# The FFN gate is computed in the preparation, and each super-tile is finished while the next one runs

## The reference

```
    g = _silu(_L0_ffn_ref(xn, L0_ffn_weight, L0_ffn_bias))
    x = x + s * g
```

## Time and profile before

| | |
|---|---|
| median of the runs | 1339.04 us |
| the profiled execution | 1338.07 us |
| its span, first to last instruction | 1336.3 us |
| mean granted TensorE clock | 0.952 |
| VectorE busy | 1224.1 us, 92% of the span |
| TensorE matmuls busy | 1133.7 us, 85% |
| ScalarE busy | 797.7 us, 60% |
| GpSimd busy | 728.3 us, 55% |

### The profile page before, as it was taken

One profiled execution on the slowest core, in us unless ns is written; L12 is line 12 of the kernel. 1 busy time (PEld: TensorE's weight loads), 2 busy tenths in 40 slices (PEclk: granted clock), 3 DMA queues, 4 the chain that ended last, 5 costly groups with the idle time before them and its releaser, 6 DMA issues. The chain is left out here.

```text
span 1336.3 us, 30910 instructions
## 1 busy us (share of the span) xinstructions
PE 1133.7 (85%) x11514; PEld 832.9 (62%) x11514; DVE 1224.1 (92%) x1945; ACT 797.7 (60%) x1226; POOL 728.3 (55%) x562
## 2 busy tenths in 40 slices
PE   4873999989999999999999999899999999999810
PEld 3742666666666666666676666666766666667600
DVE  7774999989998999999998999899989999999688
ACT  5732666656666666666666666666666666666432
POOL 4001566656665566556664666566655665666523
PEclk9865999999999999999999999999999999999955
DMA  7535332343221422342223323342224323222033
GB/s 185 176 98 127 73 73 65 69 93 85 65 65 44 106 66 66 68 112 66 63 63 74 81 66 68 66 113 57 60 51 112 66 65 69 61 57 60 19 100 89
DMA packets 68513, 105.66 MB, mean 79 GB/s; under 512 B 14051, under 2 KB 32716, under 8 KB 68044
## 3 DMA queue, kind: packets, MB, share of 16 engines
q1 hardware_dynamic: 68364, 103.68, 33.2%
HBM read 24.73 MB, written 9.96 MB: 26 GB/s over the span
## 5 line engine op out<-in xcount | busy, mean ns | idle before, releaser
L1189 POOL TENSOR_TENSOR rot<-part 128x512 f32<-128x512 f32 x256 | 382.5, 1494 | 531.9 <-DVE part L1026 480.4
L1026 DVE SCALAR_TENSOR_TENSOR part<-bcs,k_prmT,trig 128x512 f32<-128x512 f32 x512 | 500.5, 1028 | 1.4 <-DMA trig<-tri 1.3
L1138 ACT ACTIVATE E<-d 128x512 f32<-128x512 f32 x256 | 151.7, 592 | 184.1 <-PE d L846 181.5
L864 PE MATMUL s<-rot 64*128 64x128 f32 x2048 | 149.7, 285 | 23.6 <-POOL rot L1189 19.1
L1044 DVE TENSOR_TENSOR M<-s,E 128x512 f32<-128x512 f32 x256 | 163.5, 678 | 2.4 <-PE s L864 1.8
L864 PEld LDWEIGHTS s<-rot 64*128 64x128 f32 x2048 | 126.9, 188 | 62.0 <-issue 54.6
L1198 POOL TENSOR_TENSOR ce<-rot,eb 128x512 f32<-128x512 f32 x128 | 160.1, 1272 | 3.0 <-ACT eb L1160 3.0
L1220 POOL TENSOR_TENSOR sqa<-sqa,sq 128x512 f32<-128x512 f32 x112 | 142.5, 1272 | 14.2 <-ACT sq L1143 6.2
L956 PE MATMUL y<-M,xk 128*64 128x128 f32 x2048 | 140.1, 279 | 0.0
L878 PEld LDWEIGHTS o<-k_w_o,yT 128*128 128x128 f32 x1024 | 132.5, 191 | 10.4 <-DVE yT L1103 5.0
L878 PE MATMUL o<-k_w_o,yT 128*128 128x128 f32 x1024 | 134.5, 275 | 2.6 <-DVE yT L1103 2.6
(11 more groups left out here) (234 smaller groups left out, 1792.8 us busy)
## 6 DMA issues: line engine op xcount, KB each, us to landing
trig<-tri SPq DMA_DIRECT2D x512, 128.0 KB, 2.4
bcs<-bc_t SPq DMA_DIRECT2D x16, 256.0 KB, 4.0
bcs<-bc_t SPq DMA_DIRECT2D x32, 128.0 KB, 3.9
a_big<-in_L_attn_u SPq DMA_DIRECT2D x4, 512.0 KB, 6.0
xn_t<-a_xnT SPq DMA_DIRECT2D x1, 2048.0 KB, 16.4
tc_t<-a_tcT SPq DMA_DIRECT2D x1, 2048.0 KB, 15.9
bc_t<-a_tmp SPq DMA_DIRECT2D x1, 2048.0 KB, 7.5
tcs<-tc_t SPq DMA_DIRECT2D x8, 256.0 KB, 3.0
```

Of the source, the lines that this page charges most:

```text
L864: last = nc.tensor.matmul(Sp[j][:, k], rot[rows, q % 2, p, 0, k], rot[rows, q % 2, p, 1, k], start=True, stop=True)
L1026: nc.vector.scalar_tensor_tensor(out=part[:, 2 * p + f, :], in0=bcs[:, (t + q // NQ) % 2, 2 * w + f, :], scalar=col, in1=trig[:, p, 1 - f, ...
L1138: nc.scalar.activation(E[:, h % 2, :], Dp[:], ACT.Exp).then_inc(e_ready, 1)
L1189: nc.gpsimd.tensor_tensor(rot[:, q % 2, p, w, :], part[:, 2 * p, :], part[:, 2 * p + 1, :], ALU.add).then_inc(rot_ready, 1)
```

## The change

Three things change.

1. `prepare` makes the gate. VectorE takes the extremes of `xnT` and of the FFN weight between its other steps; TensorE and VectorE make the scales; the weight is quantised; at the end of the stage the eight super-tiles are scaled (ScalarE), quantised (VectorE), multiplied with the bias added by a matmul (TensorE) and put through Silu (ScalarE), and SyncE stores each gate in a DRAM tensor. The stage ends when the last gate has landed.
2. `units` finishes super-tile `t - 1` in groups 0 and 1 of super-tile `t`. The mean of squares is made and its root taken (VectorE `norm_start`, ScalarE `root`, VectorE `norm_seeded`, GpSimd `norm_refined`), ScalarE scales the projected result out of PSUM (`normalised`) in the place of the two copies, GpSimd multiplies by the gate and adds `u` (`finished`), SyncE stores in group 2 and loads the next gate and the next `u` in group 4. The last super-tile is finished behind the loop, with the last two products on VectorE. The two reductions of `xn` at `q == 2` are gone.
3. `finish` is gone, and with it the tiles `s_acc`, `ssq` and `mags`.

```diff
@@ prepare, sync
+            for t in range(NS):
+                sp.wait_ge(g_done, t + 1)
+                sp.dma_start(gate_d[t], fgate[:, t % 2, :]).then_inc(gate_stored[t % 2], 16)
             sp.wait_ge(masks_stored, 16 * 7)
+            for i in range(2):
+                sp.wait_ge(gate_stored[i], 16 * NS // 2)
@@ prepare, tensor
+            pe.wait_ge(am_done, 2)
+            nc.tensor.transpose(ps_x[1][0:2, 0:P], am[:], ident[:]).then_inc(am_t, 1)
             for g in range(4, 8):
                 linear(g)
+            pe.wait_ge(am2_done, 1)
+            nc.tensor.matmul(ps_x[1][:, 2 * P:2 * P + 2], ones[0:2, 0:P], am2[:, 0:2], start=True, stop=True).then_inc(sc_t, 1)
...
+            pe.wait_ge(left, 2)
+            for t in range(NS):
+                b = ps[2 + t % 2]
+                if t >= 2:
+                    pe.wait_ge(g_done, t - 1)
+                nc.tensor.matmul(b[:], ones[0:1, :], bias4[:], start=True, stop=False, skip_group_check=True)
+                pe.wait_ge(xq_done, t + 2)
+                for c in range(CS):
+                    last = nc.tensor.matmul(b[:, c * P:c * P + P], xq[:, t % 2, c * P:c * P + P], wq[:], start=False,
+                                            stop=c == CS - 1, skip_group_check=True)
+                last.then_inc(g_t, 1)
@@ prepare, vector
+            def extreme(b, op):
+                i = 0 if op == ALU.max else 1
+                link(nc.vector.tensor_reduce(peak[:, i, b:b + 1], xnT[:, b * L:(b + 1) * L], AX.X, op))
             for g in range(0, 8, 2):
                 dve.wait_ge(bc_squared, g + 1)
                 nc.vector.tensor_copy(big[:, 512 * g:512 * g + 512], ps[B_BANK[g]][:]).then_inc(bc_copied_v, 1)
+                extreme(g // 2, ALU.max)
...
+            extreme(0, ALU.min)
+            extreme(1, ALU.min)
             dve.wait_ge(stored[1], 16)
             dve.wait_ge(bc_done, BATCH)
             link(nc.vector.tensor_tensor(pr, big3[:, :, 0:N], big3[:, :, N:2 * N], ALU.mult))
+            dve.sem_inc(pr_done, 1)
+            extreme(2, ALU.min)
+            extreme(3, ALU.min)
...
+            link(nc.vector.tensor_scalar(sc[:, 0:2], ps_x[1][:, 2 * P:2 * P + 2], 1e-12, None, ALU.max))
+            link(nc.vector.reciprocal(sc[:, 0:2], sc[:, 0:2]))
+            link(nc.vector.tensor_scalar(sc[:, 0:2], sc[:, 0:2], FP8_MAX, None, ALU.mult))
...
+            dve.wait_ge(w_scaled, 2)
+            quantise(wq[:], wv[:, 0, :], wv[:, 1, :], P)
...
-            link(nc.vector.tensor_reduce(K["mags"][:, 2 * NS:2 * NS + 1], stage2[:, 10 * P:11 * P], AX.X, ALU.max))
-            link(nc.vector.tensor_reduce(K["mags"][:, 2 * NS + 1:2 * NS + 2], stage2[:, 10 * P:11 * P], AX.X, ALU.min))
+            for t in range(NS):
+                dve.wait_ge(xq_done, t + 1)
+                dve.wait_ge(x_scaled, 2 * t + 2)
+                if t >= 2:
+                    dve.wait_ge(g_t, t - 1)
+                quantise(xq[:, t % 2, :], fv[:, t % 2, :], fmag[:, t % 2, :], ST)
@@ prepare, scalar
+            def gate_input(t):
+                if t >= 2:
+                    act.wait_ge(xq_done, t)
+                for dst, f in ((fv, ACT.Copy), (fmag, ACT.Abs)):
+                    nc.scalar.activation(dst[:, t % 2, :], xnT[:, t * ST:(t + 1) * ST], f, scale=sc[:, 0:1]).then_inc(x_scaled, 1)
...
+            for t in range(NS):
+                if t + 2 < NS:
+                    gate_input(t + 2)
+                act.wait_ge(g_t, t + 1)
+                if t >= 2:
+                    act.wait_ge(gate_stored[t % 2], 16 * (t // 2))
+                nc.scalar.activation(fgate[:, t % 2, :], ps[2 + t % 2][:], ACT.Silu, scale=sc[:, 5:6]).then_inc(g_done, 1)
@@ units, sync
+            def load_finish(t):
+                if t > 0:
+                    sp.wait_ge(gated, t)
+                    sp.wait_ge(o_stored, 16 * t)
+                sp.dma_start(gate[:], gate_d[t]).then_inc(gate_loaded, 16)
+                sp.dma_start(by_chunk(res), u_v[t]).then_inc(res_loaded, 16)
+            def store(t):
+                sp.wait_ge(o_ready, t + 1)
+                sp.dma_start(o_v[t], by_chunk(res)).then_inc(o_stored, 16)
...
+                    if q == 2 and t > 0:
+                        store(t - 1)
+                    if q == 4:
+                        load_finish(t)
@@ units, vector
+            def norm_start(t):
+                dve.wait_ge(ssq_ready, at(1, t, 1))
+                dve.wait_ge(norm_ready, t)
+                nc.vector.tensor_scalar(nrm[:, 0, :], Dp[:, 0:CS], 1.0 / DI, EPS, ALU.mult, ALU.add).then_inc(ssq_taken, 1)
+            def norm_seeded(t):
+                dve.wait_ge(root_done, t + 1)
+                nc.vector.reciprocal(nrm[:, 1, :], nrm[:, 2, :]).then_inc(norm_seed, 1)
...
                         rotation(t, q + 1, 0, 0, 0)
+                    if q == 0 and t > 0:
+                        norm_start(t - 1)
...
                     scores(t, q, 3)
+                    if q == 0 and t > 0:
+                        norm_seeded(t - 1)
...
-                    if q == 2:
-                        dve.wait_ge(xn_loaded, (t + 1) * 16)
-                        for i, op in enumerate((ALU.max, ALU.min)):
-                            nc.vector.tensor_reduce(K["mags"][:, t * 2 + i:t * 2 + i + 1], xns[:, t % 2, :], AX.X, op).then_inc(mags_done, 1)
@@ units, scalar: root(t - 1) behind the two eb exponentials of q == 0, normalised(t - 1) behind its squares
+            def root(t):
+                act.wait_ge(ssq_taken, at(1, t, 1))
+                act.wait_ge(norm_seed, t)
+                nc.scalar.activation(nrm[:, 2, :], nrm[:, 0, :], ACT.Sqrt).then_inc(root_done, 1)
+            def normalised(t):
+                act.wait_ge(out_ready, at(T1, t, T1))
+                act.wait_ge(norm_ready, t + 1)
+                act.wait_ge(o_ready, t)
+                for c in range(CS):
+                    last = nc.scalar.activation(so[:, c * P:c * P + P], Op[:, c * P:c * P + P], ACT.Copy, scale=nrm[:, 1, c:c + 1])
+                last.then_inc(acc_done, 1)
...
-                act.wait_ge(out_ready, at(T1, t, T1))
-                nc.scalar.copy(K["s_acc"][:, t * ST:t * ST + ST], Op[:]).then_inc(acc_done, 1)
-                act.wait_ge(ssq_ready, at(1, t, 1))
-                nc.scalar.copy(K["ssq"][:, t * CS:t * CS + CS], Dp[:, 0:CS]).then_inc(ssq_taken, 1)
@@ units, gpsimd: norm_refined(t - 1) behind c_decayed of q == 0 (four instructions on 4 columns)
+            def finished(t):
+                pool.wait_ge(acc_done, at(1, t, 1))
+                pool.wait_ge(gate_loaded, 16 * (t + 1))
+                nc.gpsimd.tensor_tensor(so[:], so[:], gate[:], ALU.mult).then_inc(gated, 1)
+                pool.wait_ge(gated, t + 1)
+                pool.wait_ge(res_loaded, 16 * (t + 1))
+                nc.gpsimd.tensor_tensor(res[:], so[:], res[:], ALU.add).then_inc(o_ready, 1)
...
-                pool.wait_ge(ssq_ready, at(1, t, 0))
+                    if q == 1 and t > 0:
+                        finished(t - 1)
@@ program
-        finish(nc, K, dram[0], scratch[0], out)
```

More of the change, by code:

```diff
@@ L1112, in _ @@
                         scores(t, q + 1, 1)
+            norm_start(NS - 1)
+            norm_seeded(NS - 1)
+            dve.wait_ge(acc_done, at(1, NS, 0))
+            dve.wait_ge(gate_loaded, 16 * NS)
+            nc.vector.tensor_tensor(so[:], so[:], gate[:], ALU.mult).then_inc(gated, 1)
+            dve.wait_ge(gated, NS)
+            dve.wait_ge(res_loaded, 16 * NS)
+            nc.vector.tensor_tensor(res[:], so[:], res[:], ALU.add).then_inc(o_ready, 1)
         @block.scalar
         def _(act):
-            for s in (rounded, sin_ready, absd, e_ready, ebs_ready, sz_ready, sq_ready, acc_done, ssq_taken):
+            for s in (rounded, sin_ready, absd, e_ready, ebs_ready, sz_ready, sq_ready, acc_done):
                 act.sem_inc(s, 1)
@@ L1160, in _ @@
                         nc.scalar.activation(eb[:, p, :], Dp[:], ACT.Exp).then_inc(ebs_ready, 1)
+                    if q == 0 and t > 0:
+                        root(t - 1)
                     for p in range(2):
```

279 lines of the change are left out of this document (95 added, 184 removed).

## The result

The changed kernel takes 1305.59 us (median of 4 executions, 1304.02 to 1308.84), the kernel before 1339.39 (4 executions, 1335.22 to 1344.77) beside it. The ratio is 0.9754, with a 95% interval of 0.9733 to 0.9775: 2.5% faster. In a second series, with the changed kernel itself as an experiment, it took 1304.69 (1303.40 to 1306.37), ratio 0.9744 (0.9714 to 0.9773).

The account below looks back on a forecast made before the run. VectorE was taken to bound the loop (95% busy) and the closing stage. Span 1336.3 - 57.7 + 26.6 - 6 + 5.3 = 1304.5, so 1306 us of time; range 1296 to 1320.

Parts of the forecast that it names:

- The closing stage, -57.7: Behind the last super-tile: the closing stage shrinks to a short serial tail, gaining 57.7 us, or 53.5 with slow tiny instructions.
- The gate, +26.6: In the preparation, in front of the loop: making the gate there starts the loop 26.6 us later.
- (b): In the preparation: extremes, scales and weight quantising add 9.0 us, idle time absorbs 3.53, and 5.4 us reach L540.
- the stated bound of 32: Preparation: upper bound on the loop's later start, if the first load is not faster and the table load stays.
- The loop's gain, -6: In the loop on VectorE: two reductions removed, worth 0.78 us per super-tile, eight times, 6 us gain, 10 at most.
- The loop's additions, +5.3: In the loop, seven times: added norm, scaling, root and finishing work costs 0.75 us each, 5.3 us loss (2 to 18).
- Part 3 (e): In the loop's DMA queue: three more issues per super-tile, 0.5 us each, cost nothing; `finished` ends before the store.
- The forecast's last sentence: Prediction wrong if quantising shows gaps, seam or next group grows over 2 us, or the DMA queue waits for the store.
- A: Rival, in the loop: the Sqrt with its table load is on the path, 10.6 us over seven times, 1317; chance 0.12.
- B: Rival, in the preparation: 6.7 us per super-tile instead of 3.1, 29 us more, 1335, no change; chance 0.07.
- C: Rival, in the loop's DMA queue: group 2's store waits late, starving the rotation; slower, 1366 at half a group; chance 0.05.
- D: Rival, in the loop: more hides, reductions give 10 and additions cost 2, 1299; chance 0.10.

Follow-up runs that it names:

- the second profile: The changed kernel run again with nothing changed, profiled in an execution of 1306.37 us; median 1304.69 us, ratio 0.9744.
- the second one of before: The kernel before run once more, unchanged, as a single execution for its profile: 1339.60 us.
- both kernels with the early load: Changed kernel with the first tile loaded ahead of the gate's stores, 1302.00 us; the same with two of five quantising steps moved from VectorE to ScalarE, 1301.08 us.

## Why the prediction was right

The time was forecast at 1306, and 1305.6 and 1304.7 were measured. The mechanism held, but that the number fits to 1 us is in part luck. An execution without the early fall of the clock and without a step at the seam would take about 1303.3 (the second profile's 1306.37 less its two steps), so the sum is some 3 us too long for it, half of that in the preparation and half in the loop. The medians lie 1.4 to 2.3 us above it; this fits some executions having the fall or a step, which the forecast does not contain, but only the profiled ones show it. Point by point:

- **The closing stage, -57.7.** Measured -57.7 to -57.8. The four small GpSimd instructions take 0.20 each in the tail, spaced 0.28, 1.1 us in all, where 1.0 was taken between bounds of 0.4 and 5. (The forecast's own gain for the bound of 5 should read 53.7, not 53.5.)
- **The gate, +26.6.** Measured +25.0 in the second profile (+24.0 against the second one of before), and +30.7 and +30.9 where the clock fell early. In the second profile each link is where the sum put it: L624 ends at 100.4 (forecast 100.5), the last quantising at 125.2 (125.4; its terms add up to 125.3), the first load is issued at 129.2 (130.1) and lands in 2.7 us, 4.6 less than before (4.2), and no table load stands before the first Sin. The 4 to 6 us that two of three profiles add are no term of the sum: it took TensorE's clock as given, and between 30 and 50 us that differs from one execution to the next. They lie inside the stated bound of 32, which was set for other reasons.
- **(b) by its parts.** The counterpart of L505 starts 7.7 us later in the second profile of after (82.55 for 74.88), where the forecast's steps add up to 7.6, and L540's 5.3 later, for 5.4. Taking the extremes out gives back only 2.0 of it, since a wait of 2.7 us for TensorE's product in the scale chain then shows. The forecast did not name that wait; in the changed kernel it hides behind VectorE's other work.
- **The loop's gain, -6.** Measured 5.8, from two sides: by its removal (18.04 to 17.32, and 0.69 in super-tile 0) and by its return.
- **The loop's additions, +5.3.** Measured 3.6: 0.43 at the seam and 0.08 in group 2, seven times. `norm_start` was free, as forecast: from group 7's yT to the second rotation step it is 9.0 us into odd and 9.3 into even super-tiles in both kernels, though VectorE now waits 0.6 for the sum there and less for the angles. The seam's 0.43 has a cause that the forecast did not name. It had 0.2 for the reciprocal, 0.1 for the sines and 0.15 for the scalings, and put GpSimd's refinement at nothing in the loop without a reason. Measured are 0.09 for the reciprocal, nothing for the sines and the scalings (the kernels without root and without norm), and 0.34, what is left of 0.43, for the refinement: its four instructions take 0.6 us each beside VectorE's rotation steps and make a rotation sum late. The 0.08 of group 2 stand where the forecast had 0.3 for steps that meet `finished`.
- **What it left out, +3.1 in one profile of three.** The steps at the low clock behind the seam. Two of them made the second profile's loop +1.1 instead of -2.1, and offset half of its earlier start.
- **`finished` and the store.** GpSimd's two instructions end at 1201.72, the next rotation sum starts at 1202.34, unmoved. Part 3 (e) expected the store to find its data there; it waits 2.9 us each time, and behind it nothing is late, since the queue's wait for the rotation is 402 us as before (409). The forecast's last sentence calls the prediction wrong if the queue waits for the store. That sign did appear. It was badly chosen: the wait cost nothing here, and the step that it should have guarded, the spreading of the sines, was not late.
- **Rivals.** A fell with the root left out, B with the spacing of 3.10, C with the queue, D with the reductions at 5.8 and the loop's additions at 3.6.

## What to carry to other kernels

Price an instruction that is added to a saturated engine by the distance between two landmarks with and without it, and not by its duration: the reductions were 1.26 us long and worth 0.73. A serial stage behind a loop shrinks to its chain for the last step (64.6 us to 7.3 here) if its work fits into idle engines inside the loop; what does not fit there is paid elsewhere, here 25 us in front. Even tiny instructions placed on the engine that feeds the busiest one show up in the loop, here 0.34 us per seam. Before a few microseconds of a start-up phase are explained, profile the same kernel more than once and compare the granted clock slice by slice.

## What the runs showed of the hardware that I had not expected

- TensorE's clock can fall from 2.4 to 1.2 GHz at about 35 us in a stretch in which the profile has it busy all of the time, in two of three profiled executions of one program, and stay there for more than 10 us: 117 matmuls instead of 173 in 20 us.
- A GpSimd instruction on 128x4 elements takes 0.20 us with nothing beside it and 0.57 to 0.62 beside VectorE's 128x512 steps that read two tiles.
- The same gap of TensorE at a seam (busy 0.66 of 2.1 us) is followed by the low clock in six of 63 cases, and then costs 1.5 to 1.6 us. With the refinement on VectorE it was four of seven, at 1.4 to 2.9 us.
- Between the last instruction of `prepare` and the first matmul of `units` TensorE lost 2.7 us for which the profile shows no semaphore and no transfer, in both kernels with the early load.
